# Four transformer layers, three with experts: every expert layer scatters its result tiles to token order, and VectorE copies all expert weights

## The reference

```
x += xattn0(ln(x), ctx)          # 16 heads
x += moe0(ln(x))                 # 8 experts, top 2, gelu,  128 -> 512 -> 128
x += xattn1(ln(x), ctx)          # one head
x += moe1(ln(x))                 # 8 experts, top 2, relu,  128 -> 256 -> 128, biases
x += xattn2(ln(x), ctx)          # masked to one key each
x += conv_ffn(ln(x))             # quantised, 128 -> 512 -> 128
x += xattn3(ln(x), ctx)          # 16 heads
x += moe3(ln(x))                 # 8 experts, top 2, silu(g)*u, 128 -> 2x512 -> 128
```

## Time and profile before

| what | us |
|---|---|
| time, median of 3 runs | 735.58 (734.51 to 736.48) |
| the profiled execution: its own time | 736.1 |
| its span, first to last instruction | 734.4 |
| PE busy | 552.6 (75%) |
| PEld busy | 468.7 (64%) |
| DVE busy | 381.2 (52%) |
| POOL busy | 324.0 (44%) |
| ACT busy | 239.5 (33%) |

### The profile page before, as it was taken

The page is one execution under the profiler, slowest core; times in us unless marked ns, Lnnn a source line. Parts: engine busy times, 40 slices in busy tenths (PEclk is TensorE's granted clock), DMA queues, the critical chain, the costliest instruction groups (busy, mean ns, idle before and its releaser), DMA issues.

```text
span 734.4 us, 13330 instructions
## 1 busy us (share of the span) xinstructions
PE 552.6 (75%) x3830; PEld 468.7 (64%) x3845; DVE 381.2 (52%) x1367; ACT 239.5 (33%) x615; POOL 324.0 (44%) x435
## 2 busy tenths in 40 slices
PE   4898637999975355999864169949972299999991
PEld 2576517999963245898512147727762299899991
DVE  6888840000369754001359958887888244334335
ACT  1453104555520013565310024435420133333330
POOL 6000176837644445968450000000004688898862
PEclk9999557999965556999985569979975599999997
DMA  9945612323321012434110070030000111121124
GB/s 281 310 135 79 94 51 76 108 71 93 86 73 29 29 34 66 125 110 121 46 33 1 15 229 1 0 115 1 1 1 26 54 53 55 54 58 50 51 91 132
DMA packets 76598, 55.80 MB, mean 76 GB/s; under 512 B 9179, under 2 KB 69508, under 8 KB 76397
## 3 DMA queue, kind: packets, MB, share of 16 engines
q1 hardware_dynamic: 69965, 41.77, 20.9%
q0 software_dynamic: 6592, 13.55, 6.1%
HBM read 32.76 MB, written 22.53 MB: 75 GB/s over the span
## 4 chain that ended last, share of the span: by engine, by line
PE 49%; DVE 19%; issue 18%; POOL 8%; DMA 3%; another core or an unknown queue 2%; POOLq 1%; ACT 1%; SPq 1%; DVEq 0%; ACTq 0%
PE bank L1764 18%; PE bank L1778 11%; PE bank L1595 5%; PE bank L1750 2%; POOL XW L605 2%; POOL YG L605 2%; PE bank L1683 2%; PE bank L1652 2%; DVE XW L903 2%; POOL wcur L627 1%; DVE stats L879 1%; PE bank L1492 1%; PE bank L1672 1%; PE bank L1638 1%
## 5 line engine op out<-in xcount | busy, mean ns | idle before, releaser
L1764 PE MATMUL bank<-xT,wcur 128*128 128x128 f32 x1288 | 178.9, 284 | 2.2 <-issue 0.4
L1764 PEld LDWEIGHTS bank<-xT,wcur 128*128 128x128 f32 x1288 | 162.8, 196 | 8.2 <-issue 3.8
L591 POOL DMA_INDIRECT xw<-XW,slot_i x32 | 33.5, 1046 | 187.6 <-DVE slot_i L1068 180.3
L591 POOL DMA_INDIRECT xs<-XW,slot_i x64 | 62.6, 978 | 62.2 <-DVE slot_i L1068 37.7
L1110 DVE TENSOR_TENSOR hT<-gb,bank 128x512 f32<-128x512 f32 x46 | 31.6, 688 | 92.9 <-ACT gb L742 78.6
L1131 DVE SCALAR_TENSOR_TENSOR X<-XW,gates,X 128x128 f32<-128x128 f32 x32 | 10.3, 390 | 121.1 <-DMA XW<-ys,slot_i 121.1
L1750 PE MATMUL bank<-ident,xrow 128*128 128x128 f32 x138 | 39.7, 290 | 29.8 <-DMA xrow<-xw 18.6
L742 ACT ACTIVATE hT<-bank 128x512 f32<-128x512 f32 (+1 forms) x92 | 45.1, 490 | 42.1 <-issue 23.1
L646 POOL DMA_INDIRECT yt<-Y,dest_i x46 | 51.8, 1127 | 12.1 <-POOL dest_i L639 4.7
L754 ACT ACTIVATE Y<-bank 128x128 f32<-128x128 f32 x138 | 38.1, 277 | 53.5 <-PE bank L1778 27.2
L737 ACT ACTIVATE xT<-bank 128x128 f32<-128x128 f32 x138 | 37.6, 273 | 43.3 <-PE bank L1750 41.6
(11 more groups left out here) (325 smaller groups left out, 1154.4 us busy)
## 6 DMA issues: line engine op xcount, KB each, us to landing
xrow<-xs SPq DMA_DIRECT2D x92, 64.0 KB
ys<-Y SPq DMA_DIRECT2D x92, 64.0 KB
WA<-in_fc_dram SPq DMA_DIRECT2D x16, 256.0 KB, 4.4
xrow<-xw SPq DMA_DIRECT2D x46, 65.0 KB
xs<-zeros SPq DMA_DIRECT2D x2, 1472.0 KB, 10.6
xw<-pad_row SPq DMA_DIRECT2D x6, 390.0 KB, 10.4
WA<-in_pj_dram SPq DMA_DIRECT2D x8, 256.0 KB, 5.5
WB<-in_fc_dram SPq DMA_DIRECT2D x8, 256.0 KB, 4.7
```

Source lines behind the costliest of these rows:

```text
L591: pool.indirect_dma_start(out=dst[g], out_offset=bass.IndirectOffsetOnAxis(ap=slot_i[:, k, t:t + 1], axis=0), in_=src[:, t, :], in_offset= ...
L1764: ins = pe.matmul(dst, wcur[:, s4, at:at + P], xT[s4 % 2][:, :], start=True, stop=not L["bias"])
```

## The change

All three MoE layers take the way of layer 2.

- `ys`, `gather`, SP's stores and `combine_one` go. Each layer has a padded list `xw` of its own with 130 columns. SP lays the pads of layer 0 ahead of all expert weights (8 DMAs), those of layers 1 and 2 ahead of `experts(0)` (16 DMAs).
- DVE has one function `experts` for all layers: it copies all the weights of a tile (one copy in layers 0 and 1, two in layer 2) and computes the destinations. POOL's loop holds only scatters and puts. Four scatters of half 1 go ahead of `put(0)`, then one goes ahead of each put up to tile 12.
- SP's load of tile `t` waits for the destinations of tile `t-4` (before, in layers 0 and 1: for its transpose). After the load of tile 34 SP loads half 0's results in 4 pieces of `yt`, after tile 45 those of half 1, still inside `experts`. DVE adds half 0 in the steps 34 to 41 of its loop.
- SP's and DVE's loops are unrolled. `YT`, which took the place of `WC`, has a place of its own, as have `kbd` and `Y`.

```
+            def put(layer, t):                                       # POOL
+                s = t % RING
+                pool.wait_ge(dest_ready, layer * SLOTS + t + 1)
+                pool.wait_ge(ex_y, layer * SLOTS + t + 1)
...
+                for t in range(SLOTS):                               # POOL, experts(layer)
+                    if t < MOVES - AHEAD:
+                        scatter(GROUPS * layer + 1, t + AHEAD if t else 0, t + AHEAD + 1)
+                    put(layer, t)
...
+                sp.wait_ge(scattered[0], 16 * TOPK * GT * (layer + 1))
+                for t in range(SLOTS):                               # SP, experts(layer)
...
+                    if t >= RING:
+                        sp.wait_ge(dest_ready, base + t - RING + 1)
+                    elif layer:
+                        sp.wait_ge(dest_ready, base)
+                    load(t)
+                    if t == HALF_BACK:
...
+                        results(0)
+                results(1)
...
+                dve.wait_ge(in_experts[layer], 16 * (len(ups) + 1) * E)
+                for t in range(RING):                                # DVE, experts(layer, ups)
+                    weights(t)
+                destinations(0)
+                for t in range(SLOTS):
+                    if layer == 2:
+                        multiply(t)
                     if t + RING < SLOTS:
+                        dve.wait_ge(ex_up, base + t + 1)
+                        weights(t + RING)
+                    if t + 1 < SLOTS:
+                        destinations(t + 1)
+                    if COMBINE_AT <= t < COMBINE_AT + GT:
+                        add_result(layer, t - COMBINE_AT)
...
-            combine(0)
+            experts(0, [UP0])
             layer_norm(half(0), XN0, xn_ready)
...
             router(1, 1)
-            combine(GROUPS)
+            dve.wait_ge(in_rows, 48)
+            experts(1, [UP1])
             keys(1)
             mean_value()
             masked_result()
             dve.wait_ge(s2_evac, 2)
             split_taps()
-            combine(GROUPS + 1)
+            for c in range(TOPK):
+                combine_second(1, c)
             xattn2()
```

More of the change, by code:

```diff
@@ L388, in load_down, with lay_pads @@
                                  src[e].rearrange("(c p) d -> p c d", p=P)).then_inc(in_experts[layer], 16)
[L390 to L393, removed]
+            def lay_pads(layer):
+                for g in range(GROUPS):
+                    for s in range(RING):
+                        first = (s - g * NT) % RING
+                        sp.dma_start(xw_tiles[layer][g][first::RING].rearrange("t p d -> p t d"),
+                                     pad_row[:, s:s + 1, :].broadcast_to([P, uses(NT, first), D + 2])).then_inc(pads_out[layer], 16)
+            sp.wait_ge(pads_ready, 1)
+            lay_pads(0)
             load_up(0, UP0, fc0)
@@ L427, in experts, with load @@
[L427 to L441, removed]
+                def load(t):
+                    g = t // NT
+                    sp.dma_start(xrow[t % RING][:, :], xw_tiles[layer][g][t - g * NT]).then_inc(x_loaded[t % RING], 16)
@@ new lines, in results @@
+                def results(g):
+                    for s in range(RING):
+                        sp.wait_ge(y_put[s], 16 * (layer * uses(SLOTS, s) + uses((g + 1) * NT, s)))
+                    for i in range(g * PIECES // GROUPS, (g + 1) * PIECES // GROUPS):
+                        piece = slice(i * PT_TILES, (i + 1) * PT_TILES)
+                        sp.dma_start(YT[:, piece, :], yt_rows[:, piece, :]).then_inc(y_loaded[i], 16)
+                sp.wait_ge(scattered[0], 16 * TOPK * GT * (layer + 1))
@@ L944, in keys @@
                 else:
-                    for s in range(RING):
-                        dve.wait_ge(y_stored[s], 16 * 2 * uses(SLOTS, s))
                     link(dve.memset(bq_cols[:, :, :], 0.0))
@@ L1096, in router, with experts, weights @@
                 shares(layer, g)
-            def products():
-                def weights(t, s):
+            def experts(layer, ups):
+                base = layer * SLOTS
+                width = ups[0].shape[2]
+                def weights(t):
                     _, (e,) = nc.values_load_multi_w_load_instructions(
-                        eid_i[0:1, bass.ds(t, 1)], engines=[mybir.EngineType.DVE], min_val=0, max_val=E - 1,
+                        eid_i[0:1, t:t + 1], engines=[mybir.EngineType.DVE], min_val=0, max_val=E - 1,
@@ new lines, in combine_second @@
+            def combine_second(layer, c):
+                for i in range(PIECES // GROUPS, PIECES):
+                    dve.wait_ge(y_loaded[i], 16 * (layer + 1))
+                    for t in range(i * PT_TILES, (i + 1) * PT_TILES):
+                        ins = dve.scalar_tensor_tensor(out=X[:, t, :], in0=YT[:, t, c * D:(c + 1) * D], scalar=gates[:, c, t:t + 1],
+                                                       in1=X[:, t, :], op0=ALU.mult, op1=ALU.add)
+                link(ins)
+                if c == TOPK - 1:
+                    dve.sem_inc(half_done, 1)
```

244 lines of the change are left out of this document (59 added, 185 removed).

## The result

The changed kernel takes 742.25 us (median of 5 runs, 741.6 to 744.2), the kernel before 735.66 (5 runs, 734.51 to 736.6): a ratio of 1.0095 [1.0073, 1.0117], 6.6 us slower. The forecast was 737.6 with a range of 728.5 to 749.

The account below looks back on a forecast made before the run. PE was taken to bound the expert loops unless something holds a tile back. Terms -5.2 + 1.6 + 4.0 + 0.2 (added instruction in choices) + 1.4 gave +2.0 on 736.1, 738.1, less 0.5 for the profiled execution: 737.6, range 728.5 to 749.

Parts of the forecast that it names:

- Layer 2, -5.2: Layer 2's loop: POOL loses its copy and destinations, so the scatter-phase stall goes, -5.2 us (bounds -4 and -7.5).
- Layer 0, +1.6 up to the norm: Layer 0's loop: POOL falls behind PE for 12 tiles, so the norm starts 1.6 us later (bounds +0.3 and +5).
- SP's queue, +4.0: Behind layer 0: conv weights queue behind results(1), so DVE waits 4.0 us at weight_sums (bounds 2.5 and 5.5).
- Layer 1, +1.4: Layer 1: later start and longer loop nearly offset by the gathers' removal, +1.4 us (bounds -1.2 and +7).
- Rival 1: Layers 0 and 1: DVE copies lengthen each put at the port; 752, at half the meetings 745, named 747; chance 0.22.
- Rival 2: Losses in layers 0 and 1 covered, conv weights 1.5 sooner, layer 2 gains 6.8: 731 us; chance 0.30.
- Rival 3: Layer 1: SP's tile loads set the pace, 0.2 a tile, 9 us in all: 747 us; chance 0.06.
- 28 us of gathers give back only what the longer loop takes: Behind layer 1's loop: the gather wait goes, but PE's formerly hidden chain and DVE's masked_result then come last.

Follow-up runs that it names:

- second profile: The kernel before, unchanged, profiled once more: span 732.1 us, time 733.82 us.
- run 4: Kernel before with layer 2's part of the change alone, results still loaded and added after the loop: 730.34 us, ratio 0.9935.
- run 5: Kernel before with layer 2's part, half 0's results loaded behind tile 34 and added in steps 34 to 41: 727.89 us, ratio 0.9909.
- Run 12: Kernel of run 5 with layer 1's weight copies moved to DVE, results still gathered by POOL: 725.62 us, ratio 0.9878.
- run 1: Changed kernel with the four conv weight loads ahead of layer 0's results(1) in SP's queue: 735.72 us, ratio 1.0005.
- run 11: Changed kernel with layer 1's additions of half 0 taken out of its loop and put behind keys(1): 740.76 us, ratio 1.0071.
- run 3: Changed kernel with half 0's four piece loads issued one behind each load of tiles 34 to 37: 740.80 us, ratio 1.0072.
- run 7: Changed kernel with DVE's first four weight copies of layer 1 ahead of the router of half 1: 740.65 us, ratio 1.0088.
- run 8: Changed kernel with five edits: conv weights first, AHEAD 6, spread pieces, DVE's order behind layer 1, early copies: 727.41 us, ratio 0.9907.
- run 6: Changed kernel with DVE's work behind layer 1 reordered, split_taps and the first eight additions earlier: 742.75 us, ratio 1.0110.

## Why the prediction was right, point by point

The time lies in the range, but the change cost 6.6 where the middle of the forecast had 2.0. Against the second profile the terms are +7.7 up to SP's first load of layer 1 (forecast 5.8), +5.7 in layer 1 (1.4), +0.6 between the two layers (0) and -6.3 in layer 2 (-5.2). What failed is the size of layer 1's loop behind its first third, and the range holds the 4.6 between forecast and result only because it is wide.

**Layer 2, -5.2: right.** The steps keep 2.79. The loop gave 4.6 and the end 1.7 in the span, within the bounds, and layer 2's part alone gave 5.3 in time. Bringing half 0 back in the loop gives some 2 more over that (runs 4 and 5).

**Layer 0, +1.6 up to the norm: right**, +2.0 against the second profile. The copies wait for puts from tile 11 to 17, where 12 to 20 was forecast. The loss at the last result is 2.9, where I had 2.4.

**SP's queue, +4.0: right in kind, short in size.** The landing was forecast at 217.5 and DVE read at 217.56. That it fits so well is luck, two errors that cancel: the last result copy started at 205.78 and not at 207.4, but the last put came 1.80 behind it and not 0.45, since the last three results come 0.9 apart and a put takes 1.27. But DVE was there at 210.98, not at 213.45, because its scores came sooner, so the wait was 6.58 and the step cost 5.8 to 6.5. Since norm and queue overlap (whoever is late, the landing decides), they must be added as one: 5.8 forecast, 7.8 measured. The missing 2 is the late copy of `M` in the execution that I read: against its own `weight_sums` at 211.85 the step is 5.7.

**Layer 1, +1.4: this term was mis-sized**, +5.7. The result copies wait for puts from tile 6 on and span 74.4, forecast 72; the last addition ends 22.9 behind, forecast 23. Its parts: the start +2.1, forecast 0.9, because four copies and their register loads behind the shares cost more than what POOL's had; the loop +11.0, forecast 8.0; the stretch behind it -7.4, forecast -8.0. The first third of the loop is as forecast (put 0 to put 12: 30.6, between 30.4 without meetings and 31.4 with them). What failed is the sentence that from there PE runs 29 tiles of 1.28 less 0.6, and the piece loads cost 1.1. From the landing of put 12 to the last result copy it forecast 37.6, and 40.6 was measured. Run 12, in which no copy of the loop waits for a DMA, shows the parts:

- PE's own pace: run 12 takes 38.1 for the same 29 steps, 1.6 more than the 36.5 of the forecast. The 1.28 was read from two neighbouring transposes, the mean is 1.38 there. So of the "about 6 lost to POOL" in the kernel before, some 2 were PE's own (59.64 in run 12 against 57.6).
- The pieces: tile 29 to 34 takes 8.5 against 6.9 in run 12, so 1.7 and not 1.1 (3.8 and 3.6 in runs 1 and 11). In part it is the place in SP's queue, in part late landings (run 3).
- DVE's additions, which I had held against PE's step in layer 2 alone, need 1.67 a tile against 1.28. They cost 1.0 at the end of the loop, where I had nothing.

Between tiles 16 and 28 the changed kernel is 0.4 quicker than run 12, which closes the sum.

**Rival 1, the port, is out**: the mean put is 0.981, and 24 DMAs in a row take 1.274 each beside DVE's copies. It stood nearer than the earlier trace rows says: in the kernel before, 14 of the 46 puts took 1.33, not one. The changed kernel doesn't have this meeting. **Rival 2** was out by the queue. **Rival 3** is out: in layer 1 PE waited for `xrow` once for more than 0.3, not in each tile.

**"28 us of gathers give back only what the longer loop takes": right**, and they did not give back even that. The gathers left, 7.4 came back, since PE's setup and U's copy stand 15.1 behind the last result in the changed kernel and 15.1 and 15.8 in the two profiles of before.

## What to carry to other kernels

When a load is put into an in-order DMA queue, look at what is queued behind it, who reads that, and what that reader would otherwise wait for: here four loads in another order were worth 6.5 us. Before results are scattered tile by tile, multiply tiles by the price of one DMA on the issuing engine and set it against the loop, and do the same for each engine in each layer that gets the new work: what fits under 2.79 a tile doesn't fit under 1.28. Take an engine's step as the mean over a whole turn of its loop, and not from two neighbouring instructions. A change made of two parts (copies to another engine, a new way back) should be measured as two.

## What the runs showed of the hardware that was not expected

- A weight copy that starts inside a put costs it nothing. Put 0 of layer 1 starts at 296.86 and takes 0.97, and DVE's timeline has

```profile
296.95 0.36 DVE L992 COPY wcur<-WC 128x384 f32 x1 [1.00 <-PE bank L1671]
```

  In the earlier trace rows the copy was first, and the put took 1.33. In the changed kernel this second case is rare: no put inside the three loops takes more than 1.10.
- Two puts took 3.10 and 3.11, in two kernels, beside sixteen additions on DVE with both inputs in SBUF. Both ended 0.84 and 0.83 behind the end of the last addition (714.76 and 718.81): nearly the time of a whole put, as if it had begun only then. Other puts beside the same additions took 0.95 to 0.97, and why one is held and its neighbour is not stays open.
- The same 0.84 stands in other places. Behind layer 1's loop DVE makes four products with both inputs in SBUF, and two puts fall beside them:

```profile
371.06 2.50 DVE L837 TENSOR_TENSOR kbd<-kT,head_mask 128x512 f32<-128x512 f32 x4
```
```profile
371.21 1.39 POOL L553 DMA_INDIRECT yt<-Y,dest_i  x1 [0.31 <-issue]
...
372.90 1.50 POOL L553 DMA_INDIRECT yt<-Y,dest_i  x1 [0.30 <-issue]
```

  The second put ends 0.84 behind the last product (374.40 and 373.56). All eight other profiles with puts in layer 1 have this pair too, of 1.38 to 1.46 and of 1.49 to 1.65, the second 0.83 to 0.99 behind the products. In runs 7, 8 and 12 one scatter of POOL takes 1.75 or 1.76 beside DVE's four early copies and ends 0.84 behind the last of them.
- The Trainium skill (SBUF — State Buffer, Who interferes with whom) says that a DVE instruction with two SBUF inputs contends with a GpSimd instruction that reads SBUF. It also tells of a probe in which `tensor_tensor` did not stall a DMA, and infers the reason: the instruction takes only the shared read side, and issuing a DMA from GpSimd needs the write side. The puts of 3.1 and the pairs beside the four products speak against that inference, the short neighbours of the two for it.
- Four loads of 256 KB let puts land after 3.87 and 4.58 instead of 2.25.
- TensorE's granted clock fell to 0.50 behind layer 1 in some executions and not in others, in the kernel before in one of two (run 6).
